# Four-layer graph network on one core: VectorE's wide one-hots of a slot by one compare of two broadcast operands

## What is computed

```python
h = relu(layernorm(x)); x = x + L0(h, edge_weight, src, dst)  # 4 rounds: y = segment_sum(w * y[dst], src)
h = relu(layernorm(x)); x = x + L1(h, ...)  # message: hat basis (4x4) of two edge attributes times x_j @ W[u, v]
h = relu(layernorm(x)); x = x + L2(h, ...)  # relational convolution, twice
h = relu(layernorm(x)); x = x + L3(h, ...)  # message: silu(x_j (x) attr8 . W), then an update by node
```

## Time and profile before

| | |
|---|---|
| median of 3 runs | 18148.49 us (18147.04 to 18175.33) |
| span of the profiled execution | 18161.1 us |
| busy: PE / DVE / ACT / POOL | 15098.9 / 14620.2 / 11849.6 / 10508.1 us |
| instructions on DVE | 36172 |

### The profile page before, as it was taken

One profiled execution on the slowest core, in us unless ns is written; L12 is line 12 of the kernel. 1 busy time (PEld: TensorE's weight loads), 2 busy tenths in 40 slices (PEclk: granted clock), 3 DMA queues, 4 the chain that ended last, 5 costly groups with the idle time before them and its releaser, 6 DMA issues. The chain is left out here.

```text
span 18161.1 us, 349411 instructions
## 1 busy us (share of the span) xinstructions
PE 15098.9 (83%) x83251; PEld 13315.7 (73%) x83252; DVE 14620.2 (81%) x36172; ACT 11849.6 (65%) x23181; POOL 10508.1 (58%) x29948
## 2 busy tenths in 40 slices
PE   0148847998998999899699998999969999499997
PEld 0048846887887888789688885777747777399996
DVE  4745557887887888788699997999958888499997
ACT  2000026777777777678577777888858888377775
POOL 0458836775775775777477765666622424376610
PEclk9555558999999999999899999999989999699998
DMA  7611121010000100000211112222211212111111
GB/s 233 125 26 40 40 78 27 23 24 22 23 24 22 24 24 23 23 24 24 34 31 31 31 25 65 73 71 72 74 43 61 67 61 67 33 31 31 30 27 17
DMA packets 1268447, 826.81 MB, mean 46 GB/s; under 512 B 873458, under 2 KB 1213398, under 8 KB 1260758
## 3 DMA queue, kind: packets, MB, share of 16 engines
q1 hardware_dynamic: 880918, 671.78, 13.2%
q0 software_dynamic: 269056, 117.80, 3.5%
q10 hardware_dynamic: 118080, 33.61, 1.0%
HBM read 587.33 MB, written 235.06 MB: 45 GB/s over the span
## 5 line engine op out<-in xcount | busy, mean ns | idle before, releaser
L1548 PE MATMUL powers_sums<-powers_b_hot,powers_spread 128*128 128x224 f32 x26400 | 5284.7, 361 | 670.8 <-DVE powers_b_hot L1529 455.7
L1548 PEld LDWEIGHTS powers_sums<-powers_b_hot,powers_spread 128*128 128x128 f32 x26400 | 5097.4, 195 | 860.3 <-issue 826.7
L1650 POOL DMA_INDIRECT filled<-powers_by_b,powers_at_start x2688 | 3364.3, 1252 | 1721.6 <-issue 847.3
L2351 PE MATMUL relate_got<-relate_hot,relate_table 112*128 112x512 f32 (+1 forms) x10560 | 3091.5, 435 | 110.8 <-ACT relate_hot L2313 70.5
L1543 ACT ACTIVATE powers_b_hot<-powers_away,ones 128x672 f32<-128x672 f32 x2640 | 1977.9, 751 | 1251.6 <-PE powers_sums L1548 880.1
L1537 ACT ACTIVATE powers_away<-wide,powers_minus_b 128x224 f32<-128x224 f32 x6600 | 2717.6, 472 | 117.5 <-ACT powers_minus_b L1718 35.0
L2351 PEld LDWEIGHTS relate_got<-relate_hot,relate_table 112*128 112x128 f32 x10560 | 1702.7, 191 | 1388.5 <-issue 1315.0
L1526 DVE TENSOR_TENSOR powers_spread<-powers_a_hot,powers_message 128x640 f32<-128x640 f32 x2640 | 2154.4, 816 | 517.5 <-PE powers_sums L1548 327.8
L2313 ACT ACTIVATE relate_hot<-relate_away,ones 112x1280 f32<-112x1280 bf16 x1320 | 1797.9, 1362 | 734.3 <-PE relate_got L2351 447.3
L1529 DVE TENSOR_SCALAR powers_b_hot<-wide,powers_b_val 128x224 f32<-128x224 f32 x6600 | 1918.5, 339 | 0.0
L2366 PE MATMUL relate_mixed<-relate_mix,relate_picked 128*128 128x128 f32 x13200 | 1711.4, 277 | 107.3 <-issue 92.2
(11 more groups left out here) (475 smaller groups left out, 25622.2 us busy)
## 6 DMA issues: line engine op xcount, KB each, us to landing
relate_codes<-pair_rows SPq DMA_DIRECT2D x264, 800.0 KB
powers_given<-filled SPq DMA_DIRECT2D x528, 200.0 KB
rec<-relate_running SPq DMA_DIRECT2D x132, 400.0 KB
filled<-powers_by_b,powers_at_start POOLq DMA_INDIRECT x2688
grouped<-order_blanks POOLq DMA_DIRECT2D x20, 1320.0 KB
filled<-order_blanks SPq DMA_DIRECT2D x20, 1320.0 KB
held_recs<-grouped SPq DMA_DIRECT2D x132, 200.0 KB
conv_given<-filled SPq DMA_DIRECT2D x132, 200.0 KB
```

Of the source, the lines that this page charges most:

```text
L1548: mm = pe.matmul(gathering.sums[:, bass.ds(group * STRIDE, WINDOW)], spread[:, j].rearrange("p a d -> p (a d)"), b_hot[:, j, :], start=Fal ...
L1650: pool.indirect_dma_start(filled, bass.IndirectOffsetOnAxis(to, 0), rows, None).then_inc(spread_out[block % 2], 16)
L2351: mm = pe.matmul(got[:, n % 2, at:to], table[:, n // SLOTS % 2, half, :], flat[:, at:to], start=half == 0, stop=half == 1, skip_group_chec ...
```

## The change

In `spread_slot` the loop of `own` compares, each of the 224 columns of `wide` with one number per partition (a scalar operand), becomes one `tensor_tensor` compare over own x 224 elements. Its first operand is `b_val` of the slot's own tiles, repeated along the 224 columns; its second is `wide`, repeated over the tiles. What is written is the same. The semaphore `ready` is raised by it as by the last compare before.

```diff
     dve.tensor_tensor(spread, a_hot.unsqueeze(3).to_broadcast([P, n, 8, D]),
                       message.unsqueeze(2).to_broadcast([P, n, 8, D]), ALU.mult)
-    for j in range(own):
-        ins = dve.tensor_scalar(b_hot[:, j, :], c.wide[:], b_val[:, j:j + 1], None, ALU.is_equal)
-    ins.then_inc(ready, 1)
+    dve.tensor_tensor(b_hot[:, 0:own, :], b_val[:, 0:own].unsqueeze(2).to_broadcast([P, own, WINDOW]),
+                      c.wide[:].unsqueeze(1).to_broadcast([P, own, WINDOW]), ALU.is_equal).then_inc(ready, 1)
```

## The result

The changed kernel took 18261.58 us (median of 4 runs, 18249.48 to 18274.58) against 18147.76 us (18143.08 to 18175.33, 4 runs) for the kernel before: a ratio of 1.006, 95% interval 1.0046 to 1.0074, or +114 us. The forecast was 18,330 us, +183. The profiled execution after has a span of 18249.8 us, against 18161.1.

A forecast was written before the change was run, and what follows sets the result against it. POOL was taken to bound powers, DVE conv, and DVE and PE message. Powers +165, conv 0 and message +18 gave +183 us on the 18148.5 us median: 18,330 us, +1.0%, range 18,100 to 19,600.

The forecast's parts named there:

- POOL sets powers, and the change slows it: Powers: POOL's indirect DMAs set the time, and two-input compares close a window for them; +165 us.
- Let in at each seam: Powers: a blocked POOL DMA goes on whenever one spread or compare ends and the next follows; 1.39 instead of 1.35 us each.
- Rival 1: Powers: POOL is locked out for a whole run of slots; +2960 us there, 21.1 ms or more; chance 20%.
- the rhythm: Powers: POOL's DMAs in step with DVE's slots take 0.04 us more each, about 9 per pair; +95 us.
- the rests: Powers: after each of some 456 POOL rests a DMA waits 0.35 us at random instead of 0.20; +70 us.
- The pair after POOL's end: Powers: a pair takes 18.56 us once POOL is done, PE's pace; if that moves, the prediction is wrong.
- DVE's prices: All three stages: the new compare costs 0.534 us for 448 elements, 0.768 for 672, from start to start.
- The bound by which the whole duration counts: Conv and message: if a tensor_tensor cost its whole duration, 1320 slots would lose 0.08 us more each, 106 us.
- The counterweight: Conv: POOL's last scatters overrun 60 us of room, making conv 41 us longer instead of 39 shorter; middle taken, about 0.
- Message: Message stage: DVE's compares cost 0.534 us per slot instead of 0.507, over 660 slots; +18 us.
- the faster rival: Powers: the old compares themselves held POOL back, so 460 us could come back; 17.7 ms; chance 8%.
- Unchanged pace: POOL's pace stays, only DVE's terms in conv and message count: -39 + 18 = -21 us, 18,130 us; chance 12%.

The follow-up runs named there:

- the repeat: The changed kernel itself, unaltered, run and profiled once more beside the kernel before: 18267.53 us, ratio 1.0059.

## Why the prediction was right, point by point

**POOL sets powers, and the change slows it: right.** Undoing the change elsewhere left the whole loss (powers only). Freeing the compare of its second SBUF input took it away, with as many compares of the same length. POOL's rounds grew by 136 us in all, powers by 132.

**Let in at each seam: right but for some.** In powers the page's mean for L1649 was 1290 ns, at the very edge of the forecast 1.29 to 1.6 us. Six of 3272 transfers (six in the repeat too) started under a spread and passed seams, the longest thus:

```profile
3276.12 10.52 POOL L1649 DMA_INDIRECT filled<-powers_by_b,powers_at_start  x1 [3.21 <-issue]
```

It passed 14 seams of spreads and compares that look like any others, and ended only with the pair's slots. Together these six lost 21 us. Rival 1 is real as an event and negligible as a rate. Why these six weren't let in, stays open.

**The size: 165 forecast, 132 measured.** Hold rose by 1072 - 926 = 147 us, or 0.045 us for each of 3272 transfers. The working gave 95 us for the rhythm and 70 for the rests, 165 / 3272 = 0.050. The hold at compares grew by more (+229), and 84 us of that were made up for at spreads (-75) and scans (-9): a transfer that a compare has held seems to come out in step and to meet fewer spreads. With `wide` in PSUM the hold at spreads rose again to 267, which fits. The runs don't separate the working's two terms, so that their sum comes close is no proof of either.

**The pair after POOL's end: the warning came true, on a small scale.** The prediction said that it would be wrong if the 18.56 us moved. They did. The prediction had read one pair; before the change they alternate between 19.18 and 18.58 us. After (DVE's timeline behind POOL's first round):

```profile
4214.78 0.18 DVE L1674 TENSOR_SCALAR powers_given<-powers_first 128x32 f32 x1 [0.35 <-DVE powers_b_hot L1528]
...
4234.36 0.18 DVE L1674 TENSOR_SCALAR powers_given<-powers_first 128x32 f32 x1 [1.06 <-issue]
```

```profile
4253.31 0.18 DVE L1674 TENSOR_SCALAR powers_given<-powers_first 128x32 f32 x1 [0.35 <-DVE powers_b_hot L1528]
```

19.58 and 18.95 us, against 19.18 and 18.58 in turn before. PE was full there, as the prediction read it, but DVE stood close behind. Windows over such pairs, before and after:

```profile
8625.00:8712.00 87.00, 87.00 (x462) 86.86 (x461) 82.56 (x250) 78.29 (x165) 2.17 (x2) 1.00 0.08 21
```

```profile
4180.00:4253.00 73.00, 72.16 (x381) 71.45 (x380) 69.26 (x141) 65.24 (x137) 0.00 (x0) 1.00 0.06 17
```

PE was busy for 87.00 of 87 us and is now for 72.16 of 73. Ten slots cost DVE 10 x (0.651 - 0.615) = 0.36 us more by the quiet prices, and the pair grew by 0.38. That fits; no run tests it. With four pairs at the end of each of four rounds this is 6 us of the 132: a term that the sum left out.

**DVE's prices: right.** From start to start the new compares took 0.534 to 0.536 us (448 elements) and 0.768 to 0.769 (672), as forecast; their durations, 0.62 and 0.85, are 0.08 longer. The bound by which the whole duration counts is refuted. One reading of the prediction doesn't hold, though nothing rests on it: a scalar compare of 224 elements in 0.245 us is 1.09 ns an element, no less than the 1.045 of `tensor_tensor`, and one length can't tell a rate from a fixed part.

**Conv: the step that failed.** DVE gained what was forecast: from its first compare to its last it takes 1982.2 us instead of 2026.2, and the stage lost 38. The counterweight, POOL's end +41, was mis-sized. POOL's transfers of conv took 1232 ns on average instead of 1181, 51 ns x 1068 = +54 us of work where +101 was taken. POOL's end, counted from DVE's first compare, moved by only 37 us (1966.3 to 2003.5). It comes after DVE's last compare now, as forecast:

```profile
10995.77 0.86 POOL L1913 DMA_INDIRECT type_filled<-conv_type_rows,conv_at_start  x1 [0.30 <-issue]
```

```profile
10975.28 0.85 DVE L1528 TENSOR_TENSOR conv_b_hot<-conv_b_val,wide 128x672 f32<-128x672 f32 x1
11010.50 1.79 DVE L2775 TENSOR_TENSOR X<-X,Y 128x1568 f32<-128x1568 f32 x1 [34.37 <-PEq L99]
```

But DVE's idle time ahead of the layer's end was 29.05 us before and is 34.37, 5 us more, not 80. Against DVE's last compare POOL's end went from 61 us ahead to 20 behind, 81 us, more than the 60 of room. It cost little because behind DVE's last compare PE, ACT and a load finish the stage's sums anyway: DVE's idle time there is 29.0 us in all four profiles with scalar compares in conv, where POOL is done 58 to 79 us ahead. The prediction counted each microsecond of POOL past DVE's last compare as lost, and so left this overlap out. In the nine other profiles with the new compare in conv POOL's end lies 25 to 41 us behind and the idle time is 36.5 to 50.7 us, 50.7 in the repeat: there POOL takes back up to 22 us of DVE's gain.

**Message: +18 forecast, +14 measured,** and 14 came back with the scalar compares.

**Rivals.** The compares of before held 33 us in powers, not 460: the faster rival's premise is refuted. Whether they ran in the two-port mode that it supposes, no run shows. *Unchanged pace* is refuted by powers alone. The sum, 132 - 38 + 14 = +108, is 75 us under the forecast: 38 of that in conv, 33 in powers, 4 in message.

## What to carry to other kernels

Before merging DVE instructions next to a POOL that issues indirect DMAs, count the SBUF inputs of the merged one: a scalar-operand compare has one, a `tensor_tensor` two, and a POOL that bounds the stage pays for the second (262 us of hold against 33). Moving a small constant operand to PSUM keeps the single instruction and removes the hold (262 us to 6). And look for the largest hold, not the newest: here the scans held 650 us. Freeing them and the compares, with denser rests, took 292 us from powers (335 from the kernel, with conv's gain), where the change had cost 114. The denser rests are the part whose need wasn't tested.

## What the runs showed that I had not expected

- POOL can be too free. With its transfers unheld and 1.26 us apart PE's matmuls came 0.71 or 1.42 us apart, 1085 times in powers, and the kernel lost 1164 us. A rest after 3 transfers instead of 6 brought that to 79. Part of what holds at spreads and scans cost POOL was thus a pause that PE needed. What PE lacks meanwhile stays open. The trace gives no sign of slower fetching of instructions: the DMA queue for them moved 89 packets in powers here and 90 in the kernel before, which took 0.44 and 0.46 us on average.
- The long distances differ by chip for one code (220 and 400 with the same powers), and with them the time of powers by 131 us. This is one profile each. The freed scans don't end it: their powers took 5825 us with 211 long distances on the second chip and 5734 with 49 on the third.
- Transfers passing up to 14 seams between spreads and compares: six in each of two profiles of the changed kernel, 21 and 27 us.
